# A four-layer graph network on one core: attentions end in parts of 64, 32 and 28 tiles, their end pieces fused, unused visits dropped

## The reference, cut to what matters

```python
x = _layernorm(x + _L0_gnn_ref(x, src, dst, ...))
x = _layernorm(x + _L1_gnn_ref(x, ..., src, dst, edge_type_8))
x = _layernorm(x + _L2_gnn_ref(x, src, dst, ...))
x = _layernorm(x + _L3_gnn_ref(x, edge_attr_64, src, dst, ...))
...
attn = ex / denom[dst]
msg = hn[src] * attn[:, :, None]
out = jax.ops.segment_sum(msg, dst, num_segments=n)
out = out.reshape(n, H * D) + bias
out = out + inputs_node
```

## Time and profile before

| | |
|---|---|
| median of 3 runs | 9217.67 us (9209.52 to 9221.89) |
| profiled execution, its own time | 9211.23 us |
| its span | 9209.4 us |
| POOL busy | 6461.5 us, 70% |
| PE busy | 3897.9 us, 42% |
| ACT busy | 3149.7 us, 34% |
| DVE busy | 1367.5 us, 15% |
| granted PE clock over the span | 0.508 |
| gathers | 2 x 3328, about 2.5 us each from issue to landing |

### The profile page before, as it was taken

The page is one execution under the profiler, slowest core; times in us unless marked ns, Lnnn a source line. Parts: engine busy times, 40 slices in busy tenths (PEclk is TensorE's granted clock), DMA queues, the critical chain, the costliest instruction groups (busy, mean ns, idle before and its releaser), DMA issues. The chain is left out here.

```text
span 9209.4 us, 87314 instructions
## 1 busy us (share of the span) xinstructions
PE 3897.9 (42%) x18631; PEld 3698.9 (40%) x18636; DVE 1367.5 (15%) x2919; ACT 3149.7 (34%) x8588; POOL 6461.5 (70%) x6800
## 2 busy tenths in 40 slices
PE   6456565656522342424433333333340433424334
PEld 6456555656422332423433333333330433424334
DVE  8100000000330101101320000000022111111125
ACT  1343434344322442524014343434330433424320
POOL 1677777777477777777747777777756777777774
PEclk7555555555555555555555555555555555555555
DMA  2322222222221111111111111111113111111111
GB/s 58 93 55 52 55 56 55 51 55 56 87 49 27 27 27 26 27 27 27 27 23 26 26 26 26 26 26 26 26 21 73 31 31 31 31 31 31 31 31 23
DMA packets 313922, 353.35 MB, mean 38 GB/s; under 512 B 155871, under 2 KB 188741, under 8 KB 310315
## 3 DMA queue, kind: packets, MB, share of 16 engines
q0 software_dynamic: 218064, 232.48, 14.8%
q1 hardware_dynamic: 95632, 117.96, 4.0%
HBM read 310.23 MB, written 42.24 MB: 38 GB/s over the span
## 5 line engine op out<-in xcount | busy, mean ns | idle before, releaser
L771 POOL DMA_INDIRECT rows_l<-table,idx_c_l x3328 | 3140.0, 944 | 1307.6 <-issue 1013.6
L952 POOL DMA_INDIRECT rows_a<-table,idx_c_a x3200 | 3052.2, 954 | 1047.9 <-issue 1047.9
L566 PE MATMUL acc_l<-rows_l,hot_l 128*128 128x65 f32 x6656 | 1495.1, 415 | 1960.3 <-DMA rows_l<-table,idx_c_l 1906.7
L566 PEld LDWEIGHTS acc_l<-rows_l,hot_l 128*128 128x128 f32 x6656 | 1467.4, 332 | 1995.3 <-issue 1995.3
L566 PE MATMUL acc_a<-msg_a,hot_a 128*128 128x66 f32 (+1 forms) x6656 | 1486.0, 423 | 438.1 <-DVE msg_a L1049 229.6
L566 PEld LDWEIGHTS acc_a<-msg_a,hot_a 128*128 128x128 f32 x6656 | 1440.4, 331 | 488.0 <-issue 476.8
L700 ACT ACTIVATE dist_l<-iota,neg_c_l 128x128 bf16<-128x128 f32 x3328 | 1052.0, 386 | 30.9 <-PE acc_l L566 25.5
L700 ACT ACTIVATE dist_a<-iota,neg_c_a 128x128 bf16<-128x128 f32 x2816 | 890.1, 386 | 150.3 <-PE acc_a L566 150.3
L906 ACT ACTIVATE score_a<-score_a 128x128 f32<-128x128 f32 (+1 forms) x28 | 13.1, 469 | 2577.2 <-DVE score_a L1018 2577.2
L1086 PE MATMUL work_a<-ident,rows_a 128*128 128x128 f32 (+1 forms) x70 | 22.4, 444 | 2000.1 <-DMA rows_a<-table,idx_c_a 1985.0
L733 ACT COPY idx_c_l<-src_tl 128x16 int32 (+1 forms) x208 | 42.3, 204 | 2416.9 <-PE acc_l L566 2391.1
(11 more groups left out here) (256 smaller groups left out, 2269.7 us busy)
## 6 DMA issues: line engine op xcount, KB each, us to landing
rows_l<-table,idx_c_l POOLq DMA_INDIRECT x3328, 2.5
rows_a<-table,idx_c_a POOLq DMA_INDIRECT x3328, 2.5
feat<-edge_attr SPq DMA_DIRECT2D x25, 1125.0 KB
feat<-edge_attr SPq DMA_DIRECT2D x25, 937.5 KB
table<-stage SPq DMA_DIRECT2D x49, 260.0 KB, 2.1
spread<-zero SPq DMA_DIRECT2D x12, 832.0 KB, 14.1
starts_l<-spread SPq DMA_DIRECT2D x2, 3328.0 KB, 11.6
target<-target_d SPq DMA_DIRECT2D x5, 832.0 KB, 9.3
```

Source lines behind the costliest of these rows:

```text
L566: return nc.tensor.matmul(acc[:, bass.ds(at, row.shape[-1])], hot, row, start=False, stop=True, skip_group_check=True)
L771: pool.indirect_dma_start(rows[:, s, k, 0:D], None, table, bass.IndirectOffsetOnAxis(idx_c[:, s, k:k + 1], 0)).then_inc(gathered[s], 16)
L952: pool.indirect_dma_start(rows[:, u, k, 0:row], None, table, bass.IndirectOffsetOnAxis(idx_c[:, u, k:k + 1], 0)).then_inc(gathered[u], 16)
```

## The change

- In all four passes the last four visits (1660 to 1663), which no edge uses, are left out: `VU = T + NB - 1`. In the plain passes the last body is written out behind the loop, and its last slot of 12 is waited for and visited by fours (`gathered_last`). The edge units of layer 0 are placed in the first 48 visits of each body instead of all 64.
- The last attention group is cut in parts of 64, 32 and 28 visits (`LAST`), each with its own chain.
- In these parts PE reads the first 32 places behind the score transposes instead of before the wait for the gathers.
- ACT makes all one-hot tiles, in the last two groups too, and in every group the first 16 (RING) before the exponentials.
- The end of an attention is one piece in the same block: counts, reciprocal and multiplication are read straight from PSUM into the buffer of the gathered rows, the node blocks go in parts of 28 and 21 (`PARTS`), the squares are made on ACT, ACT's table for the square root is loaded ahead, and each part has its own store. The residual and bias of layer 3 are added ahead of the pass, as 2 * xcur + bias.

```diff
+VU = T + NB - 1
...
         def steps(engine, body):
-            body(0, True)
-            with engine.Fori(1, ITERS) as i:
-                body(i, False)
+            body(0, True, CH)
+            with engine.Fori(1, ITERS - 1) as i:
+                body(i, False, CH)
+            body(ITERS - 1, False, CH - (V - VU))
...
-            at = [u * BODY // UNITS for u in range(UNITS)]
+            at = [u * (BODY - CH) // UNITS for u in range(UNITS)]
...
-                                pe.wait_ge(gathered[s], 16 * CH * (i + 1))
-                                for k in range(CH):
+                                if not last:
+                                    pe.wait_ge(gathered[s], 16 * CH * (i + 1))
+                                for k in range(end if last else CH):
                                     n = s * CH + k
+                                    if last and k % QUAD == 0:
+                                        pe.wait_ge(gathered_last[k], 16 * QUAD)
...
+            LAST = (0, P // 2), (P // 2, 3 * P // 4), (3 * P // 4, VU - (G - 1) * P)
...
+                PARTS = (0, NG // 2 + 1), (NG // 2 + 1, NG)
...
-                    body(G - 1, 0, G // 2, False, G - 1, 0, HALF)
-                    body(G - 1, 0, G // 2, False, G, HALF, P)
+                    for n, (q0, q1) in enumerate(LAST):
+                        body(G - 1, 0, G // 2, False, G - 1 + n, q0, q1)
...
-                            exps(g, first)
-                            if not (isinstance(g, int) and g >= G - 2):
-                                hots(g, u, first)
+                            act.wait_ge(chunk_ready, COLUMNS * (g + 1))
+                            hots(g, u, first, q0, q0 + RING)
+                            exps(g if turn is None else turn, first)
+                            hots(g, u, first, q0 + RING, q1)
...
+                        nc.scalar.sqrt(warm[:], ones[:, 0:1])
+                        for n in range(len(PARTS)):
+                            act.wait_ge(centred, n + 1)
+                            b0, b1 = (b * BPB for b in PARTS[n])
+                            nc.scalar.activation(square[:, b0:b1], y[:, b0:b1], ACT.Square).then_inc(squared, 1)
...
+                        for n in range(len(PARTS)):
+                            sp.wait_ge(x_ready, n + 1)
+                            done = result_out(sp, PARTS[n][0] * BPB, PARTS[n][1] * BPB, x_out)
+                        sp.wait_ge(x_out, done)
...
+                        if own_row is not None:
+                            dve.wait_ge(own_in, 16)
+                            nc.vector.scalar_tensor_tensor(xcur[:], xcur[:], 2.0, own_s..., ALU.mult, ALU.add)
...
-                                if late:
-                                    for n in range(k, k + PIECE):
-                                        if n % QUAD == 0:
-                                            dve.wait_ge(summed, 1 + g * (P // QUAD) + (n - RING) // QUAD + 1)
-                                        ins = nc.vector.tensor_scalar(hot[:, n % RING], iota[:], neg_c[:, u, n:n + 1], 0.0, ALU.add, ALU.is_equal)
...
-                        keep_sums(dve, acc, summed, kept, sums)
+                        for n, (n0, n1) in enumerate(PARTS):
+                            for k in range(n0, n1):
+                                last = nc.vector.tensor_tensor(y[:, kb]..., sums_of[:, k, :, 0:sums]..., count[:, :, kb]..., ALU.mult)
+                            link(nc.vector.tensor_tensor(y[:, b], y[:, b], xcur[:, b], ALU.add))
+                            link(nc.vector.reduce_sum(mean[:, b], y[:, b], AX))
+                            link(nc.vector.tensor_scalar(mean[:, b], mean[:, b], 1.0 / D, None, ALU.mult))
+                            nc.vector.tensor_tensor(y[:, b], y[:, b], along(mean[:, b], D), ALU.subtract).then_inc(centred, 1)
...
-                            places = {lo: offsets(g, lo) for lo in range(q0, q0 + EARLY * CH, CH)}
+                            early = range(q0, min(q0 + EARLY * CH, q1), CH)
+                            places = {lo: offsets(g, lo) for lo in early if not late}
...
+                            places.update((lo, offsets(g, lo)) for lo in early if late)
```

174 lines of the change are left out of this document (92 added, 82 removed).

## The result

The changed kernel takes 9155.97 us (median, 9150.85 to 9157.10) against 9217.48 us before: the ratio is 0.9932, with a 95% interval of 0.9920 to 0.9944. The forecast was 9162 us in a range of 9144 to 9186. The profiled execution took 9156.46 us, its span is 9154.7 us, 54.7 us shorter than before. The medians differ by 61.5 us, 6.5 more than the 55.0 of the forecast: the traced execution of the kernel before (9211.2) was 6 us faster than its median.

What follows compares the result with a forecast made beforehand. GpSimd's tile gathers at 1.25 us each bound the kernel, so only dropped gathers and GpSimd's idle stretches could win time. 13 + (8.2 + 7.1 + 1.6) + 10.3 + (-2.0 + 15.2 + 1.6) = 55.0 us off 9217.7 gave 9162, range 9144 to 9186.

Steps and rivals of the forecast that it cites:

- Layer 0's end, 13: First plain pass: dropped gathers and no edge units in the last 16 visits shorten the end by 13 us.
- at worst 2.6: First plain pass: PE may reach the last landing late because it still reads places, costing at worst 2.6 us.
- Layer 1's PE, 8.2: First attention: with the last group in three parts, PE's visits end 8.2 us sooner.
- 3.7 us of queued visits: Late parts: place reads of 11.4 us run 3.7 us ahead of queued visits where one transpose stands before them.
- (a): Rival: place reads are not hidden behind queued visits, 16.4 us lost over both attentions, 9179 us; chance 0.15.
- The ends, 7.1 and 15.2: Last visit to the end of the last pass: 7.1 us won in the first attention, 15.2 in the second.
- the stores, 1.6 each: Store of each attention cut in two: the first piece's head start wins 1.6 us per attention.
- Layer 2's end, 10.3: Second plain pass: last landing 5.0 us sooner and 4 visits behind it instead of 16, 10.3 us won.
- Layer 3's PE, -2.0: Second attention: a third chain of about 24 us makes the visits end 2.0 us later.
- (b): Rival: more is won, as plain-pass landings trail less and stores scale with bytes, 5 and 7 us, 9150; chance 0.10.
- (c): Rival: no change that can be told, the split costs another chain per attention, 37 us together, 9199; chance 0.05.
- (d): Rival: slower, gathers written out behind the plain passes' loops run slow, costing 110 us, 9272; chance 0.04.

Runs made afterwards that it cites:

- whole slot: Changed kernel, but in both plain passes the last slot of 12 gathers is waited for as a whole instead of by fours; 9174.89 us, ratio 0.9951.
- units: Changed kernel with the eleven edge units of a plain body spread over all 64 visits again instead of the first 48; 9164.61 us, ratio 0.9945.
- the kernel with only the fused end: Kernel before plus only the new end of the attentions and its stores, all 1664 visits and two halves kept; 9198.25 us, ratio 0.9978.
- with pieces: Changed kernel with the residual and bias pass ahead of the second attention's groups made in seven pieces instead of one instruction; 9161.98 us, ratio 0.9938.

## Why the prediction was right, and where it was not

**Layer 0's end, 13, measured 12.2.** The visits by fours, the moved units and the shorter pass are each real (whole slot: 1.5 us; units: 4.1 us), but three sizes were off and cancel. The pass of gathers was 4.0 us shorter, not 5.0. The last gather lands 3.0 us after its start instead of 4.8 (2345.78 to 2350.62 before), which the forecast did not have. And PE comes 2.4 us late, where the forecast took 0.7 of its "at worst 2.6": the copies begin 6.2 us behind that landing instead of 3.8. The quicker landing goes with the dropped gathers: in the kernel with only the fused end, which still makes them, the last four of this pass land after 3.7, 3.9, 4.7 and 4.7 us, and those ahead of them after 2.4 to 3.2. Why these four are slow is open.

**Layer 1's PE, 8.2, measured 7.7.** The chain was followed part for part, each start of visits held to 0.6 us against the last gather, and it leaves 45.49 us behind the last gather as worked out. The missing 0.5 us is that the way to that gather was 4.5 us shorter instead of 5.0. Two parts instead of three cost 10.6 us with the reads behind the scores. That the reads are hidden by 3.7 us of queued visits, which decided between the forecast and rival (a), was right: scores to tails take 8.0 and 8.1 us with one transpose queued (7.7) and 8.6 with four (11.4 - 3.0 = 8.4).

**The ends, 7.1 and 15.2, measured 7.3 and 15.5, and the stores, 1.6 each, measured 1.7 and 1.8.** The fused end alone gave the same numbers, and one store took 1.76 and 1.78 us back. Two terms of the sum for the ends had no row, 1.2 for small operations and 1.0 for starts and links. The small operations took 1.3 us, and the five passes 3.6 us each, cut in two, instead of 3.42, which makes 0.8.

**Layer 2's end, 10.3, measured 10.9.** Four visits behind the last landing, and the whole slot took 3.6 us of it back. Here too two sizes cancel: the pass was 4.0 us shorter instead of 5.0, and PE saw the last landing 3.2 us after the last gather's start instead of 4.9. With the whole slot waited for it was still 3.3, so that is not the counting by fours.

**Layer 3's PE, -2.0, measured -7.7. This is the term that was off.** It has three pieces. From the head gather to group 11's scores it took 5.1 us longer (before 1981.0, after 1986.0); group 11 took 0.3 us less, where the forecast had 0.9; group 12, from the end of group 11's visits, took 132.0 us instead of 129.0, 3.0 more where the forecast had 2.9. So the step that failed is the sentence that the two added passes "are done as one ahead of group 0, where PE waits for 128 gathers, over 100 us". PE's wait was the wrong cover: the pass lies on DVE beside the first gather, and it is GpSimd that it holds. One gather took 3.94 us, and 3.0 us of the 5.1 are that one; with pieces it is gone. The other 2.1 us lie in POOL's busy time as well (1464.2 us up to group 12 instead of 1459.0, with 519.4 us of idle time in both): 0.8 in single gathers of 1.1 to 1.2 us among the first 128, the rest spread thinly over the pass. A part of them is scatter between executions (from the first gather of rows to the first of group 12, ten traces with the whole pass in one piece have 1981.2 to 1984.9 us, three with pieces or without the pass 1978.9 to 1981.0, and before it was 1978.4). What the rest is stays open.

**A gain of 4.4 us that no step had.** The node layers between layer 0 and layer 1 took 136.3 us in the changed kernel's trace, 140.8 before, and 136.9 to 150.3 in the experiments, none of which touches them. It can't be credited to the change: it goes with the granted clock there, 0.70 in the one trace and 0.65 in the other (see the end). The total of 54.7 us against a forecast of 55.0 is therefore closer than the steps earned: without these 4.4 us it would have been 50.3. That closeness is luck.

**The rivals.** (a), reads not hidden, fell by the gaps above. (b), more won, fell: a store is worth its head start. The last landings did trail less, by 1.7 to 1.8 us in each plain pass, but that goes with the dropped gathers and not with the counting. (c) was right in one of the two attentions: the third part costs 6.4 to 6.9 us in layer 3, which the forecast had seen only as "2.0 us lost" against the kernel before, not against a cut in two. (d), slow gathers where they are written out, fell: the 60 written out in the attention took 953 ns each, as the 1600 in the loop and behind it (rows above), and the plain passes' gathers took the 1.25 us each that they took before.

## What to carry to other kernels

When a chain is cut to overlap with landings, every further part repeats the chain's fixed cost. Whether the cut pays depends on that cost (18.7 us from scores to visits with one head, 24.7 with four here), and the best number of parts differs between two uses of the same code. A pass that one engine does "while another waits" has to be set against all engines that work at that time, above all the one that sets the pace; cut into short pieces, it cost that one nearly nothing. Reads that stand ahead of a wait are free if the wait is long, and dear if it isn't: put only as many into the chain as the next step needs.
